# Cross-attention scores: query and key projections with 64-row products instead of a folded query-key matrix

## What is computed

```python
x   = layer_norm(context)          # 120 rows per sequence
lat = layer_norm(latents)          # 128 rows per sequence
q = lat @ Wq                       # (64, 128, 16*64)
k, v = split(concatenate([x, lat], axis=1) @ Wkv, 2)
dots = einsum('bhid,bhjd->bhij', q, k) * 64 ** -0.5
attn = softmax(dots, axis=-1)      # over 248 keys
out  = einsum('bhij,bhjd->bhid', attn, v)
return merged_heads(out) @ Wout
```

## Time and profile before

| | us |
|---|---|
| median of 3 runs | 2010.41 (2010.4 to 2011.98) |
| the profiled execution | 2021.62 |
| its span, first to last instruction | 2019.9 |
| PE busy in the span | 1950.3 (97%) |
| DVE, ACT, POOL busy | 1494.0, 1279.6, 1289.2 |
| mean granted TensorE clock | 0.987 of full speed |

### The profile page before, as it was taken

How to read it: one execution, slowest core, us unless ns; L and a number is a source line. 1 busy time by engine, 2 the same in 40 slices (tenths; PEclk the granted TensorE clock), 3 DMA queues, 4 the chain that set the end, 5 groups by cost and what they waited for, 6 DMA issues and landing times. The chain is left out here.

```text
span 2019.9 us, 47365 instructions
## 1 busy us (share of the span) xinstructions
PE 1950.3 (97%) x15995; PEld 1686.7 (84%) x15995; DVE 1494.0 (74%) x3901; ACT 1279.6 (63%) x3929; POOL 1289.2 (64%) x1461
## 2 busy tenths in 40 slices
PE   7999979999999999999999999999999988999997
PEld 4555569999999999999999999899999877888875
DVE  5999956777777777777777778777777755655675
ACT  3777656666666666666666666666666644555565
POOL 4888856666666666666666666666666555444674
PEclk9999989999999999999999999999999988999999
DMA  4301000000000000000000000000000011232454
GB/s 123 84 19 29 19 19 1 17 16 17 16 14 21 15 17 16 16 14 22 16 17 16 15 20 29 24 17 16 15 21 11 12 41 58 85 86 79 128 147 140
DMA packets 103984, 75.27 MB, mean 37 GB/s; under 512 B 10998, under 2 KB 97638, under 8 KB 103622
## 3 DMA queue, kind: packets, MB, share of 16 engines
q1 hardware_dynamic: 94806, 54.20, 9.7%
q0 software_dynamic: 8640, 17.97, 2.5%
q10 hardware_dynamic: 304, 0.07, 0.0%
HBM read 39.64 MB, written 32.57 MB: 36 GB/s over the span
## 5 line engine op out<-in xcount | busy, mean ns | idle before, releaser
L1201 POOL TENSOR_TENSOR x_prob<-x_prob,x_inv 128x496 f32<-128x496 f32 x512 | 520.6, 1017 | 458.9 <-DVE x_inv L1320 456.2
L1266 ACT ACTIVATE x_prob<-x_ps_S,x_nmax 128x248 f32<-128x248 f32 x1024 | 472.0, 468 | 223.4 <-DVE x_nmax L1314 221.5
L1314 DVE TENSOR_REDUCE x_nmax<-x_ps_S 128x2 f32<-128x496 f32 x512 | 343.2, 670 | 103.6 <-PE x_ps_S L1072 95.8
L1281 ACT COPY x_probT<-x_ps_T 124x512 f32<-124x512 f32 x512 | 300.8, 588 | 166.7 <-PE x_ps_T L1463 164.4
L1463 PE MATMUL x_ps_T<-ident,x_prob 128*124 128x128 f32 x2048 | 319.2, 278 | 8.7 <-POOL x_prob L1201 7.1
L1070 PE MATMUL x_ps_S<-first_kT_lo,x_G_hi 128*128 128x248 f32 x1024 | 327.1, 319 | 0.0
L1463 PEld LDWEIGHTS x_ps_T<-ident,x_prob 128*124 128x124 f32 x2048 | 232.9, 140 | 75.2 <-POOL x_prob L1201 29.1
L1072 PE MATMUL x_ps_S<-first_kT_hi,x_G_hi 128*128 128x248 f32 x1024 | 284.1, 277 | 0.0
L1071 PE MATMUL x_ps_S<-first_kT_hi,x_G_lo 128*128 128x248 f32 x1024 | 284.0, 277 | 0.0
L1433 PE MATMUL x_ps_O<-x_probT,x_V 124*64 124x128 f32 x4096 | 252.4, 276 | 0.7 <-issue 0.7
L1300 DVE TENSOR_TENSOR x_G_lo<-x_ps_G,x_G_hi 128x512 fp32r<-128x512 f32 x256 | 176.0, 688 | 88.6 <-ACT x_G_hi L1260 88.6
(11 more groups left out here) (263 smaller groups left out, 4428.2 us busy)
## 6 DMA issues: line engine op xcount, KB each, us to landing
w_wkv<-sorted_rows SPq DMA_DIRECT2D x142, 66.0 KB
e_back<-sorted_results SPq DMA_DIRECT2D x32, 256.0 KB
latents<-first_nlat SPq DMA_DIRECT2D x32, 128.0 KB, 1.8
turned_rows<-w_rows SPq DMA_DIRECT2D x32, 128.0 KB, 1.7
w_wq<-turned_rows SPq DMA_DIRECT2D x32, 128.0 KB
out_dram<-e_result SPq DMA_DIRECT2D x16, 256.0 KB
first_nk<-latents SPq DMA_DIRECT2D x32, 124.0 KB
first_nk<-in_ctx SPq DMA_DIRECT2D x32, 120.0 KB, 2.2
```

The lines of the kernel that those rows point to most:

```text
L1201: nc.gpsimd.tensor_tensor(prob[:, k], prob[:, k], inv[:, k].unsqueeze(2).broadcast_to([P, 2, K]), ALU.mult).then_inc(prob_ready, 1)
L1266: nc.scalar.activation(prob[:, k, h, :], ps_S[:, n % BANKS, h * K:(h + 1) * K], ACT.Exp, bias=nmax[:, k, h:h + 1], accum_out=total[:, k, h ...
L1281: nc.scalar.copy(probT[0:KT, s % (2 * GANG)], ps_T[0:KT, s % 2, :]).then_inc(probT_ready, 1)
L1314: nc.vector.tensor_reduce(nmax[:, k, :], ps_S[:, n % BANKS, 0:2 * K].rearrange("p (h k) -> p h k", h=2), AX, ALU.max, negate=True).then_in ...
```

## The change

The folded matrix goes. The weights Wq (with the scale 1/8) and Wk are split into high and low parts instead, by two ACT and two DVE instructions of 1024 columns in the tail of `linear_attention`; the transposes and products of the weights go with the PSUM bank views they used.

In the rounds `make_G` is replaced by two functions. `make_k` computes for each j the keys of two heads and both sequences (2 x 64 rows, three matmuls of 496 columns). `make_q` computes for each two j the queries (six matmuls of 256 columns). Both write `ps_G`, one after the other, and are split by `k_hi`, `q_hi` on ACT and `k_lo`, `q_lo` on DVE. `scores` contracts over the 64 rows of one head: a call computes head 1 of unit n (rows 64 to 127, bank n % 3) and head 0 of unit n+1 (rows 0 to 63, the next bank), their six matmuls interleaved. So unit n+1 is begun one step earlier than before, and PE waits for the exponentials of the unit that used its bank. Two of the four `outT` copies of a round move from DVE to ACT, and the pieces of the routing on DVE are cut anew. `kT_full` moves into the columns of `later.wq` that are free by then. The start of the block is ordered anew over more banks.

```diff
-            def make_G(pair, keys_par, j):
-                for h in range(2):
-                    last = split_product(nc, ps_G[:, h * 256:(h + 1) * 256], [m[:, 2 * j + h, :] for m in M_part],
+            def make_q(keys_par, jj, bank=ps_G[:]):
+                for n in range(2):
+                    at = (jj * 2 + n) * P
+                    last = split_product(nc, bank[:, n * 256:(n + 1) * 256], [w[:, at:at + P] for w in wq_part],
                                          [k[:, keys_par, :, C:K] for k in kT_part])
-                last.then_inc(G_psum, 1)
+                last.then_inc(q_psum, 1)
+            def make_k(keys_par, j, bank=ps_G[:]):
+                split_product(nc, bank[:, 0:2 * K], [w[:, j * P:(j + 1) * P] for w in wk_part],
+                              [k[:, keys_par].rearrange("p u k -> p (u k)") for k in kT_part]).then_inc(k_psum, 1)
...
-            def scores(k, u, keys_par, pair):
-                for h in range(2):
-                    last = split_product(nc, ps_S[:, k, h * K:(h + 1) * K], [g[:, pair, h, u, :] for g in G_part],
-                                         [t[:, keys_par, u, :] for t in kT_part])
-                last.then_inc(S_psum, 1)
+            def scores(n):
+                wait(pe, first_head, n + 1)
+                heads = [(n + odd, 1 - odd) for odd in range(2) if 0 <= n + odd < ROUNDS * UNITS]
+                for part, (q_n, k_n) in enumerate(((0, 1), (1, 0), (0, 0))):
+                    for unit, h in heads:
+                        j, u, rows = unit % UNITS // 2, unit % 2, slice(h * DH, (h + 1) * DH)
+                        last = nc.tensor.matmul(ps_S[:, unit % BANKS, h * K:(h + 1) * K],
+                                                q_part[q_n][rows, j // 2 % 2, j % 2, u, :], k_part[k_n][rows, j % 2, u, :],
+                                                start=(part == 0), stop=(part == 2))
+                        if h and part == 2:
+                            last.then_inc(S_psum, 1)
+                        elif part == 2:
+                            last.then_inc(first_head, 1)
...
+                    if unit + s + LEAD + 1 < ROUNDS * UNITS:
+                        pe.wait_ge(exp_ready, (unit + s + 2) * 2)
+                        if u == 0:
+                            pe.wait_ge(k_lo_ready, r * PAIRS + j + 3)
+                        if s % 4 == 0:
+                            pe.wait_ge(q_lo_ready, r * PAIRS // 2 + s // 4 + 2)
+                    if unit + s + LEAD < ROUNDS * UNITS:
+                        scores(unit + s + LEAD)
...
                     if u == 0 and (r < FINAL or ahead < PAIRS):
-                        pe.wait_ge(G_lo_ready, r * PAIRS + ahead)
+                        if s % 4 == 2:
+                            wait(pe, q_lo_ready, min(r * PAIRS // 2 + s // 4 + 3, ROUNDS * PAIRS // 2))
...
-                        make_G(ahead % 2, par if ahead < PAIRS else 1 - par, ahead % PAIRS)
+                        make_k(par if ahead < PAIRS else 1 - par, ahead % PAIRS)
+                    ahead = s // 4 + 2
+                    if s % 4 == 1 and (r < FINAL or ahead < PAIRS // 2):
+                        pe.wait_ge(k_lo_ready, r * PAIRS + j + 4)
...
+                        make_q(par if ahead < PAIRS // 2 else 1 - par, ahead % (PAIRS // 2))
...
# DVE's step s
+                    ahead = s // 4 + 2
+                    if s % 4 == 2 and (r < FINAL or ahead < PAIRS // 2):
+                        q_lo(r * PAIRS // 2 + ahead)
...
-                        G_lo(r * PAIRS + j + 3, (j + 3) % 2)
-                    if s % GANG == 1 and (s > 1 or later_round(r)):
+                        k_lo(r * PAIRS + j + 3)
+                    if s == 9 or (s == 1 and r) or (s == 13 and r == FINAL):
                         out_copy(r * GANGS + s // GANG - 1, (s // GANG - 1) % GANGS)
...
-            ROUTE = {11: (0, 2), 13: (2, 6), 14: (6, 11), 15: (11, 17)}
-            ROUTE_LATE = {3: (RANK_STEP, SLOT_STEP), 6: (SLOT_STEP, 22), 8: (22, STEPS)}
+            ROUTE = {11: (0, 2), 13: (2, 6), 14: (6, 8), 15: (8, 13)}
+            ROUTE_LATE = {0: (13, 15), 1: (15, RANK_STEP), 3: (RANK_STEP, SLOT_STEP), 6: (SLOT_STEP, 22), 8: (22, STEPS)}
...
# ACT's step s
-                        G_hi(r * PAIRS + ahead, ahead % 2)
+                        k_hi(r * PAIRS + ahead)
+                    ahead = s // 4 + 2
+                    if s % 4 == 1 and (r < FINAL or ahead < PAIRS // 2):
+                        q_hi(r * PAIRS // 2 + ahead)
+                    if s % 8 == 7 and (s == 7 or r < FINAL):
+                        out_copy(r * GANGS + s // 4 - 1)
```

More of the change, by code:

```diff
@@ L592, in keys_lo @@
                                      ALU.subtract).then_inc(self.kT_lo_ready, 1)
[L594 to L620, removed]
@@ L699, in linear_attention @@
         nlat, lat_stored = first.nlat, first.lat_stored
-        first.wqT, first.wkT = room.sbuf("wqT", [P, 8, D]), room.sbuf("wkT", [P, 8, D])
         ps_t = room.psum("ps_t", [P, 512])
@@ L726, in linear_attention @@
         block = stack.enter_context(nc.Block())
-        free = [ps_cum[:, n // 2, n % 2 * 512:n % 2 * 512 + 512] for n in range(4)]
         def here(s):
@@ L862, in step @@
                 if t == PAIRS:
-                    for n in range(3):
-                        first.turned_weights(act, ps_qk, n)
-                if t == PAIRS + 1:
-                    for n in range(4):
-                        first.M_hi(act, free[n], n)
+                    for n in range(2):
+                        first.wqk_hi(act, n)
                 if here(t):
@@ L962, in step @@
                 if t == PAIRS + 1:
-                    for n in range(3):
-                        first.M_lo(dve, free[n], n)
+                    for n in range(2):
+                        first.wqk_lo(dve, n)
                 if t == PAIRS + 2:
                     first.keys(dve, ps_qk, 0)
-                    first.M_lo(dve, free[3], 3)
                     first.wv_lo(dve)
@@ L1031, in step @@
                     last.then_inc(vy_psum, 1)
-                if t == PAIRS:
+                if t == PAIRS + 2:
                     pe.wait_ge(pos_ready, PAIRS)
-                    pe.wait_ge(later.attention_loaded, 48)
-                    first.turn_weights(pe, ps_qk, ident, 0)
-                if t == PAIRS + 1:
-                    first.turn_weights(pe, ps_qk, ident, 3)
-                    for n in range(2):
-                        pe.wait_ge(cum_taken, 2 * PAIRS - 1 + n)
-                        first.products(pe, free[n * 2:n * 2 + 2], n)
-                if t == PAIRS + 2:
                     first.turn_keys(pe, ps_qk, ident, 0, 0)
@@ L1257, in _, with q_hi, k_hi, out_copy @@
         def _(act):
-            def G_hi(n, pair):
-                act.wait_ge(G_psum, n + 1)
-                nc.scalar.copy(G_part[0][:, pair], ps_G[:]).then_inc(G_hi_ready, 1)
+            def q_hi(n, bank=ps_G[:]):
+                act.wait_ge(q_psum, n + 1)
+                nc.scalar.copy(q_part[0][:, n % 2], bank).then_inc(q_hi_ready, 1)
+            def k_hi(n, bank=ps_G[:]):
+                act.wait_ge(k_psum, n + 1)
+                nc.scalar.copy(k_part[0][:, n % 2].rearrange("p u k -> p (u k)"), bank[:, 0:2 * K]).then_inc(k_hi_ready, 1)
+            def out_copy(n):
+                act.wait_ge(O_psum, n + 1)
+                nc.scalar.copy(outT[:, n % GANGS].rearrange("p j u q -> p (j u q)"), ps_O[:]).then_inc(outT_ready, 1)
             def exponentials(n, k):
@@ L1506, in _ @@
             pe.wait_ge(kT_lo_ready, 1)
[L1507 to L1520 removed]
+            make_q(0, 0, ps_T[:, 0, :])
+            make_k(0, 0)
+            make_V(0, 0, 0, 0)
+            make_k(0, 1, ps_T[:, 1, :])
+            pe.wait_ge(V_ready, 1)
+            make_V(0, 0, 0, 1)
+            pe.wait_ge(q_lo_ready, 1)
+            pe.wait_ge(k_lo_ready, 1)
+            scores(-1)
+            pe.wait_ge(weights_ready, 4)
+            make_q(0, 1, ps_O[:])
+            scores(0)
+            pe.wait_ge(V_ready, 2)
+            make_V(0, 0, 1, 0)
+            pe.wait_ge(k_lo_ready, 2)
+            scores(1)
+            make_k(0, 2)
+            pe.wait_ge(V_ready, 3)
+            make_V(0, 0, 1, 1)
+            pe.wait_ge(exp_ready, 2)
+            scores(2)
             pe.wait_ge(set_ready, SETS)
```

145 lines of the change are left out of this document (72 added, 73 removed).

## The result

The changed kernel takes 2097.74 us (median of 4 runs, 2096.88 to 2098.12), the kernel before 2011.2 us on the same chip (4 runs, 2010.4 to 2013.0). The ratio is 1.0427, 95% interval 1.0415 to 1.0439: 86.5 us slower. The forecast was slower, 2081 us, in a range of 1995 to 2130. Sign and range held; of its four terms two were wrong, by more than 40 us each and in opposite directions, so that the nearness of 2081 is for the most part luck.

What follows compares the result with a forecast made beforehand. The prediction took PE's instruction stream to bound the kernel. Products +77, scores -31, stalls +28 and start -3 gave +71 us on the median 2010.4, so 2081 us, in a range of 1995 to 2130.

Steps and rivals of the forecast that it cites:

- Keys and queries for G: PE in the rounds: keys and queries products cost 8.15 us a round against 5.7 for G, about +77 us.
- the start: Start of the block: weight transposes, products and copies go, four 1024-column instructions come; -3 us, between 0 and -8.
- The scores: PE's 512 score steps: 64-row halves overlap but pay a 0.40 us round trip; 1.08 against 1.14 us, 31 us saved.
- (a): PE's switch to 64 rows and back is cheap, 0.20 instead of 0.40 us: +6 us; ends 1950 to 2015, chance 0.18.
- (b): PE's scores: the row halves do not overlap in this form, 1.45 us a step, 2253 us; chance 0.06.
- The border of 0.26: Row-mode switch price on PE, in us, below which the change was said to be faster, with the stalls as counted.
- The stalls: PE waits on the DVE and POOL chain behind `q_lo`, steps 6 and 14: 1.2 against 0.3 us a round, +28 us.
- Rival (c): DVE's and ACT's queues are late everywhere: stalls 3 us a round, 96 us instead of 28, 2149 us; chance 0.14.

Runs made afterwards that it cites:

- the kernel with full rows and the old cut: The changed kernel with scores over all 128 rows and the old cut of DVE's routing pieces: 2100.19 us, ratio 1.0413.
- the square: Four versions of the changed kernel, ratios with new and old routing cut: scores over 128 rows 1.0321 and 1.0413, over 64 rows 1.0427 and 1.0486.
- the experiment that used it up: The changed kernel with one more unused DVE reduction ahead of each `q_lo`, 128 in all: 2156.32 us, ratio 1.0681.
- run 704: Not a run or kernel: a count, the two DVE lines L403 and L395 execute 704 times in the traces of the eleven kernels.

## Why the prediction was right and wrong

- **Keys and queries for G, +77 us: right.** The products have the starts that were counted: 0.22 to 0.23 for a 496-column matmul of the keys, 0.115 for the queries' (the 59 of 61 us above). In the trace of the kernel with full rows and the old cut these products hold PE for 255.7 us of the thirty rounds, G held it for 179.9 before: 2.53 us a round, where +2.5 was counted, and 81 us in 32 rounds. That kernel is 83 us slower; 81, less 3 for the start, plus 9 for the transposes (21.2 us lost instead of 11.9) and less 6 ahead of L312 are 81. This alone decided the sign.
- **The scores, -31 us: the step that failed.** "0.36 transposes + 0.20 in + 0.32 scores + 0.20 out = 1.08" measured 0.36 + 0.27 + 0.345 + 0.20 = 1.17. The way out was as forecast (0.09 late, 0.11 for the product's first load). The way in was mis-sized: 0.17 late instead of 0.10, and 0.105 for the uncovered load. The 0.10 came from a 64-row matmul behind four loads and matmuls of another kind; behind these transposes it is more; why is open. The three pairs take 0.115 each, 0.345 in all, where six at 0.054 were 0.32. Worth -31 in the forecast, it was +15 by the timeline (0.03 x 512) and +15 to +21 by the square: an error of 46 to 52 us.
- **Rivals (a) and (b): refuted by the same timeline.** The round trip costs 0.35 us and more instead of 0.20 or nothing, and the loads are not done ahead: each step shows PEld idle for 0.17 ahead of the scores, and the first load and its matmul start together (at 914.88 in the step above). The border of 0.26 that the prediction gives for rival (a) leaves out the +37 us of stalls which (a) itself adds; with them it would be about 0.18, and (a)'s own 0.20 gave +6. The Trainium skill, "TensorEngine Tiling (Array Packing)", Key Properties, says that a change of mode drains TensorE; the trace agrees: 0.17 us without a load on the way in, and 0.09 late on the way out, though how much of each is the draining is not told apart. And the halves overlap, even when the program does not interleave them.
- **The stalls, +28 us: the second step that failed; they fell by 15 us.** Between the transposes of step 6 and those of step 8, `q_lo` ended at 0.82 us (0.84 forecast) and V copy at 1.42 (1.5), so the places were right. Then the three routing pieces took 0.5 instead of 0.9: L395 is 0.18 us long, not 0.59. DVE's starts come 0.61 apart for instructions of 0.68, for which the count had 0.66 to 0.69. POOL ended at 3.69 instead of 4.25. And PE was ready at 3.71 instead of 3.5 (its last matmul ahead starts at 940.55, the next place is 0.23 later), since its steps are longer by the missed 0.1 each; the transposes start at 3.75. 0.8 us of stall became 0.04 there. Over all rounds PE lost 2.6 us at the transposes where it had lost 11.9, and nothing ahead of L312 where it had lost 5.8. PEld's idle time on POOL was 0.3 us a round, where 1.2 was forecast. In step 14 the new cut did what the forecast gave it, and more: without it PEld's waits are 26.2 us (64 rows) or 32.0 (128 rows), and PE loses 15.1 or 21.2 us. The 12 to 19 us that the cut is worth were inside the change, and the forecast had only counted it as two pieces instead of five.
- **Rival (c): refuted.** It wanted 3 us of stalls a round. From 400 to 1600 us PEld waits for no engine but POOL, 8.5 us, if the 0.17 of each change of rows is left aside. The nearest limit is the 0.25 us behind `q_lo`, by the experiment that used it up.
- **Why 2081 was close: mostly luck.** Forecast were +77 - 31 + 28 - 3 = +71. By PE's starts and the square it was 81 for the products, about 20 for the scores (0.04 x 512), -15 for the stalls and -3 for the start, +83, and +86 was measured. The scores were forecast 51 us too low and the stalls 43 too high. The two are not wholly independent: each step that is 0.1 longer gives the chain on DVE 0.1 more. But with the same cut the 64-row steps took only 3 us (5.8 to 2.6) or 6 us (21.2 to 15.1) from the transposes' loss; the rest of the offset is chance. The predicted round of 44.5 to 45 us was 45.7, the step of 1.7 to 1.8 us was 1.87.

What stays open: what of the 0.17 us on the way in is emptying the array and what is taking up the new rows; no row tells the two apart. Nor was a kernel with more banks of scores tried, in which one trip would serve two units without the wait.

## What to carry to other kernels

Half-row matmuls that run two heads at once must pay for going into 64 rows and back: here three pairs saved 0.35 us of stream, and the trip between 128-row work took 0.35 to 0.38 more than the 128-row form pays at its own borders. By these prices a run of four pairs or more would gain (an estimate from these numbers; no run here had a longer one without a wait in it). Count the price of both borders at each step, from a kernel's own starts with the same operation on either side, ahead of the gain inside. And where a change takes a product apart that was folded ahead of the loop, count the columns that come into the loop first: here they decided the sign, whatever the scores did.

A small difference inside a change can be worth as much as one of its main terms: the move of some small pieces by a step or two was worth 12 to 19 us, about what the 64-row scores cost. With the two moved `outT` copies it makes the kernel before the fastest version, 0.9965.

## What the runs showed of the hardware

Row halves keep their own order: with the three matmuls of one half behind the three of the other in the program, the first of both start together (907.21), and the time is the same (1.0429 and 1.0427).

A wait of PE for its own matmuls, in the middle of a run of the same form, costs 0.37 us from start to start instead of 0.115, and 0.105 more because the load behind it is not done ahead.

The length of a small DVE instruction can depend on what POOL does beside it. L403 on 128x2 elements has a median of 1158 ns in the kernel before (150 at its shortest) and 151 ns in the changed one. DVE and POOL in the kernel before:

```profile
903.67 1.25 POOL L591 TENSOR_TENSOR first_kT_lo<-first_kT_full,first_kT_hi 128x496 fp32r<-128x496 f32 x1
903.76 1.17 DVE L403 SCALAR_TENSOR_TENSOR slots_col<-slots_col 128x2 f32<-128x2 f32 x1
```

They end at 904.92 and 904.93. Likewise L395 at 899.42 ends at 900.01, 0.06 behind a POOL instruction of 898.94 to 899.95, and three rounds in a row show it so. In the changed kernel all 32 of L395 take 0.18, and 27 of the 32 of L403 take 0.15. In the traces of the eleven kernels the two lines run 704 times, and 266 of these are long. Every long one starts while a POOL TENSOR_TENSOR runs and ends 12 to 22 ns (L403) or 43 to 50 ns (L395) behind its end; no short one starts inside one that has more than 0.134 us left. Not every DVE instruction does so: L405, a RECIPROCAL on 128x2 elements, starts 198 times with more than 0.2 us of such a POOL instruction left and never takes more than 0.169. So the two DVE instructions last until POOL's is over. That POOL's holds them is the plain reading; the places changed with the kernels, and no run moved one of the two alone. The duration of a small instruction in a profile is then worth little for a sum once its neighbours move: the forecast's 0.9 for three routing pieces had 0.4 of this in it.
